# Attention in single hops beside the quantised weight pieces, x and constants issued by SyncE, and another order in the last tile

## The reference, cut to what matters

```python
# layer 0, conditioning: 8 blocks of 32 steps are summed
block_repr = inputs.reshape(B, n_blocks, block_size, H).sum(axis=2)
keys = einsum(block_repr, Wk); keys = keys / rms(keys) * rms_weight
scores = einsum(keys, q); attn = softmax(scores)          # over the blocks
attended = einsum(attn, block_repr)
x0 = layernorm(inputs + attended @ Wo.T) * ln_gamma + ln_beta
# layer 0, feed-forward: activations and weights quantised in blocks of 32
gate, up = q_act(x0) @ q_w(w_gate).T, q_act(x0) @ q_w(w_up).T
x = x + q_act(silu(gate) * up) @ q_w(w_down).T
# layer 1: a GRU over the 256 steps, then a linear layer with a router over 16 experts of rank 16
gi = x_t @ W_ih + b_ih; gh = h @ W_hh + b_hh
r, z = sigmoid(i_r + h_r), sigmoid(i_z + h_z); n = tanh(i_n + r * h_n); h = (1 - z) * n + z * h
out = h @ W.T + bias + sum over the top 2 experts of share * (h @ A.T) @ B.T
x = x + out
```

## Time and profile before

| | us |
|---|---|
| median of 3 runs | 1797.59 |
| lowest, highest | 1797.26, 1799.63 |
| the profiled execution | 1797.46 |
| its span in the trace | 1795.7 |
| busy: PE (matmul) | 1588.7 (88%) |
| busy: DVE | 1448.9 (81%) |
| busy: ACT | 684.1 (38%) |
| busy: POOL | 502.6 (28%) |

### The profile page before, as it was taken

How to read it: one execution, slowest core, us unless ns; L and a number is a source line. 1 busy time by engine, 2 the same in 40 slices (tenths; PEclk the granted TensorE clock), 3 DMA queues, 4 the chain that set the end, 5 groups by cost and what they waited for, 6 DMA issues and landing times.

```text
span 1795.7 us, 76317 instructions
## 1 busy us (share of the span) xinstructions
PE 1588.7 (88%) x32908; PEld 1243.1 (69%) x32908; DVE 1448.9 (81%) x5603; ACT 684.1 (38%) x1736; POOL 502.6 (28%) x572
## 2 busy tenths in 40 slices
PE   5531458999999999999999999999999999999986
PEld 2211126778777777778778777777778777878874
DVE  6968888888888888888888888888888888887654
ACT  2323224444433443444443344443444434443331
POOL 4645323222222222222222222222222222221001
PEclk8755679999999999999999999999999999999996
DMA  8413300000101000001000000000010100000000
GB/s 301 156 66 112 138 18 20 26 33 32 33 32 32 32 32 32 22 19 33 32 32 33 32 33 32 32 28 31 33 33 32 32 32 32 27 27 26 21 15 19
DMA packets 35409, 80.10 MB, mean 45 GB/s; under 512 B 4864, under 2 KB 5248, under 8 KB 34688
## 3 DMA queue, kind: packets, MB, share of 16 engines
q1 hardware_dynamic: 28080, 63.09, 10.3%
q10 hardware_dynamic: 6992, 12.13, 1.9%
HBM read 58.43 MB, written 16.78 MB: 42 GB/s over the span
## 4 chain that ended last, share of the span: by engine, by line
PE 75%; DVE 18%; issue 3%; ACT 2%; POOL 1%; DMA 1%; ACTq 1%; DVEq 0%; SPq 0%; POOLq 0%
PE ps_rn_turn L1274 23%; PE ps_gi L1168 11%; PE ps_z L1274 10%; PE ps_gate_up L1107 6%; PE ps_down L1125 6%; PE ps_base L1177 4%; PE ps_gate_up L1101 4%; PE ps_base L1221 3%; PE ps_route L1177 3%; DVE fe L784 1%; DVE gi L583 1%; DVE gi L585 1%; DVE ps_rn_turn L581 1%; PE ps_rn_turn L1116 1%; DVE ps_gi L566 1%
## 5 line engine op out<-in xcount | busy, mean ns | idle before, releaser
L1274 PE MATMUL ps_rn_turn<-hT,whh 128*128 128x32 f16 x16320 | 449.2, 176 | 37.2 <-DVE hT L722 37.1
L1274 PEld LDWEIGHTS ps_rn_turn<-hT,whh 128*128 128x128 f16 x16320 | 435.2, 96 | 63.8 <-DVE hT L722 56.8
L996 POOL TENSOR_TENSOR qf<-f8c,fe 128x512 bf16<-128x512 bf16 x128 | 135.6, 1059 | 887.2 <-DVE f8c L801 867.3
L1168 PE MATMUL ps_gi<-x1T,wih 128*128 128x128 f16 x4608 | 288.6, 219 | 1.2 <-ACT gi L537 1.2
L1168 PEld LDWEIGHTS ps_gi<-x1T,wih 128*128 128x128 f16 x4608 | 270.2, 98 | 25.6 <-issue 1.7
L546 ACT ACTIVATE r_tanh<-r_pre,scale_half 128x64 f32<-128x64 f32 x256 | 89.0, 348 | 459.2 <-DVE r_pre L742 459.2
L1274 PE MATMUL ps_z<-hT,whh 128*128 128x32 f16 x8160 | 243.2, 176 | 0.0
L1274 PEld LDWEIGHTS ps_z<-hT,whh 128*128 128x128 f16 x8160 | 222.7, 96 | 0.0
L537 ACT ACTIVATE gi<-ps_gi,b_i,scale_x 128x128 f32<-128x128 f32 x384 | 144.4, 456 | 193.2 <-PE ps_gi L1168 193.2
L736 DVE TENSOR_TENSOR r_half<-ps_rn_turn,gi 128x64 f32<-128x64 f32 x256 | 56.5, 221 | 137.9 <-PE ps_rn_turn L1274 137.7
L548 ACT ACTIVATE z_tanh<-z_pre,scale_half 128x64 f32<-128x64 f32 x256 | 89.0, 348 | 159.4 <-DVE z_pre L752 159.4
(11 more groups left out here) (196 smaller groups left out, 2604.5 us busy)
## 6 DMA issues: line engine op xcount, KB each, us to landing
wih<-in_x_steps ACTq DMA_DIRECT2D x32, 256.0 KB, 5.4
xin<-in_x_steps SPq DMA_DIRECT2D x32, 256.0 KB, 3.8
xres<-in_x_steps SPq DMA_DIRECT2D x32, 256.0 KB, 3.2
x_dram<-x SPq DMA_DIRECT2D x32, 256.0 KB, 2.2
x_in<-x_dram SPq DMA_DIRECT2D x32, 256.0 KB, 2.8
out_rows<-y SPq DMA_DIRECT2D x32, 256.0 KB, 2.0
wst<-in_ffn_w SPq DMA_DIRECT2D x12, 512.0 KB, 3.3
sg_gs<-in_ffn_w SPq DMA_DIRECT2D x12, 512.0 KB, 3.8
```

The lines of the kernel that those rows point to most:

```text
L996: g.tensor_tensor(blocked(qf[:, :]), blocked(f8c[:, :]), spread(fe16[:, :]), ALU.mult).then_inc(qf_done, 1)
L1168: last = mm(ps_gi[:, j * P:(j + 1) * P], wih_parts[:, k, at:at + P], x1T[:, x, k, :], start=k + w + x == 0, stop=k == KD - 1 and w == 1)
L1274: last = mm(ps[:, (at + j) * 2 * B:(at + j + 1) * 2 * B], whh[:, k, u, gate * D + j * P:gate * D + (j + 1) * P], hx(t)[:, 2 * k:2 * k + 2, ...
```

## The change

- `over_pieces` has one order for all engines: beside piece p the block sums for p < 8, attention step p-8 for p from 8 to 17 (ten steps), slot (-4, p-18) after that; slots 6 and 7 of c = -4 after the last piece. On ScalarE and SyncE the piece comes first (`piece_first=True`), on the others the work beside it.
- SyncE issues the x tiles (`load_x`), with the same waits on `summed`, and, with piece 4, the constants, `WkT` and `WoT`. ScalarE keeps only the two first constants. The copy to `br` becomes the first attention step of ScalarE.
- Attention has ten steps, one dependent hop in each.
- VectorE's first pass over a piece also waits for its own third pass over the piece before (`w_q`).
- GpSimd's `x_bias` goes from s = 5 to s = 3.
- In the last tile (no R) the base matmuls go from s = 4 and 6 to s = 0 and 3.

```diff
-        def over_pieces(piece, sums, attention, slot, ahead=0):
-            for p in range(SUM_PARTS):
-                sums(p)
-                piece(p // 2, p % 2)
-            for p in range(SUM_PARTS, PIECES // 2):
-                piece(p // 2, p % 2)
-            done = 0
-            for p in range(PIECES // 2, PIECES):
-                upto = min(p - PIECES // 2 + 1 + ahead, 12)
-                for beside in range(done, upto):
-                    if beside < 6:
-                        attention(beside)
-                    else:
-                        slot(-4, beside - 6)
-                    if beside == 11:
-                        slot(-4, 6)
-                        slot(-4, 7)
-                done = upto
-                piece(p // 2, p % 2)
+        def over_pieces(piece, sums, attention, slot, piece_first=False):
+            for p in range(PIECES):
+                if piece_first:
+                    piece(p // 2, p % 2)
+                if p < SUM_PARTS:
+                    sums(p)
+                elif p < SUM_PARTS + ATTENTION:
+                    attention(p - SUM_PARTS)
+                else:
+                    slot(-4, p - SUM_PARTS - ATTENTION)
+                if not piece_first:
+                    piece(p // 2, p % 2)
+            for s in range(PIECES - SUM_PARTS - ATTENTION, STEPS):
+                slot(-4, s)
...
# SyncE
+            def load_x(p):
+                first = (p + 1) * TILES // SUM_PARTS if p else 0
+                for t in range(first, min((p + 2) * TILES // SUM_PARTS, TILES)):
+                    wait(sp, summed, t - XRING + 1)
+                    sp.dma_start(xtile[t % XRING], x_steps[t * P:(t + 1) * P, :]).then_inc(xt_loaded[t % XRING], 16)
+                if p == 4:
...
+                    for dst, src in small:
+                        sp.dma_start(dst, src).then_inc(consts, 16)
+                    sp.dma_start(wk_sb, WkT).then_inc(wkwo_loaded, 16)
+                    sp.dma_start(wo_sb, WoT).then_inc(wkwo_loaded, 16)
-            over_pieces(piece, nothing, nothing, slot)
+            over_pieces(piece, load_x, nothing, slot, piece_first=True)
...
# ScalarE
-            def load_x(p):
...
-                if p == SUM_PARTS - 1:
-                    act.wait_ge(summed, TILES)
-                    nc.scalar.activation(br, ps_down[:, :], ACT.Copy).then_inc(at_act, 1)
             def attention(step):
                 if step == 0:
+                    act.wait_ge(summed, TILES)
+                    nc.scalar.activation(br, ps_down[:, :], ACT.Copy).then_inc(at_act, 1)
+                if step == 1:
                     act.wait_ge(at_pe, 1)
...
-            over_pieces(piece, load_x, attention, slot, ahead=1)
+            over_pieces(piece, nothing, attention, slot, piece_first=True)
...
# VectorE: piece, and the steps of attention (2, 3, 4, 5 become 4, 5, 6, 7)
                 dve.wait_ge(w_abs_ok, count_piece(turn, u, 1))
+                wait(dve, w_q, count_piece(turn, u))
...
# GpSimd (rinv: step 2 becomes 5)
+                if L and s == 3:
+                    pool.wait_ge(x1in_loaded, count(l, 16, 16))
+                    wait(pool, y_ok, count(l, 1))
+                    g.tensor_tensor(x1_bias[:, :], x1_in[:, :], bias_b[:, :], ALU.add).then_inc(x1b_done, 1)
                 if L and s == 5:
...
-                    pool.wait_ge(x1in_loaded, count(l, 16, 16))
-                    wait(pool, y_ok, count(l, 1))
-                    g.tensor_tensor(x1_bias[:, :], x1_in[:, :], bias_b[:, :], ALU.add).then_inc(x1b_done, 1)
...
# TensorE (steps 0, 1, 3, 4, 5 become 1, 2, 5, 6, 7, and the product with WoT step 8)
+            base_parts_at_end = {0: (0,), 3: (1, 2, 3)}
...
                 if L:
-                    for k in base_parts.get(s, ()):
+                    for k in (base_parts if R else base_parts_at_end).get(s, ()):
                         base(l, k)
...
-            over_pieces(piece, block_sums, attention, slot, ahead=1)
+            over_pieces(piece, block_sums, attention, slot)
```

More of the change, by code:

```diff
@@ L50 @@
 SUM_PARTS = 8
+ATTENTION = 10
 PIECE = 1024
@@ L335, in piece @@
                 sp.dma_start(wst[u][:, :], ffn_w[at:at + P, :]).then_inc(w_loaded[u], 16)
+            def load_x(p):
[4 more added lines that the diff above has]
+                if p == 4:
+                    small = [(maskA[:, :], block_mask), (rw_b, rms_w.partition_broadcast(P)),
+                             (q_b, query.partition_broadcast(P)), (iota_b[:, :], iota.partition_broadcast(P)),
+                             (gamma_b[:, :], gamma.partition_broadcast(P)), (beta_b[:, :], beta.partition_broadcast(P)),
+                             (bias_b[:, :], bias.partition_broadcast(P)), (b_i[:, :], b_ih), (b_h[:, :], b_hh),
+                             (rb1_b[:, :], rb1.partition_broadcast(P)),
+                             (rb2_b[:, :], rb2[0:EXPERTS].partition_broadcast(P)),
+                             (gates_b[:, :], gates.partition_broadcast(P)), (rw2_sb[:, :], rw2T)]
+                    assert len(small) == CONSTS
+                    for dst, src in small:
+                        sp.dma_start(dst, src).then_inc(consts, 16)
+                    sp.dma_start(wk_sb, WkT).then_inc(wkwo_loaded, 16)
+                    sp.dma_start(wo_sb, WoT).then_inc(wkwo_loaded, 16)
             def loads(c):
@@ L443, in attention @@
                 if step == 0:
+                    act.wait_ge(summed, TILES)
+                    nc.scalar.activation(br, ps_down[:, :], ACT.Copy).then_inc(at_act, 1)
+                if step == 1:
                     act.wait_ge(at_pe, 1)
                     nc.scalar.activation(brT, ps_route[:, :], ACT.Copy).then_inc(at_act, 1)
[L446 removed]
+                if step == 3:
                     act.wait_ge(at_pe, 2)
                     nc.scalar.activation(keys, ps_base[:, :], ACT.Copy).then_inc(at_act, 1)
[L449 removed]
+                if step == 5:
                     act.wait_ge(at_dve, 8)
                     nc.scalar.activation(row[1], row[0], ACT.Exp).then_inc(at_act, 1)
[L452 removed]
+                if step == 6:
                     act.wait_ge(at_pe, 4)
                     nc.scalar.activation(acol[:, :], ps_base[:, 0:1], ACT.Copy).then_inc(at_act, 1)
[L455 to L460 removed]
+                if step == 7:
+                    act.wait_ge(at_pe, 5)
+                    nc.scalar.activation(attT[:, :], ps_route[:, :], ACT.Copy).then_inc(at_act, 1)
+                if step == 9:
+                    act.wait_ge(at_pe, 6)
+                    nc.scalar.activation(proj[:, :], ps_base[:, :], ACT.Copy).then_inc(at_act, 1)
             def weights(c, s):
@@ L595, in attention @@
                     v.tensor_tensor(b_i[:, 0:2 * KD], b_i[:, 0:2 * KD], b_h[:, 0:2 * KD], ALU.add).then_inc(c_dve, 1)
-                if step == 2:
+                if step == 4:
                     dve.wait_ge(at_act, 3)
@@ L604, in attention @@
                     v.reduce_sum(dot[:, :], kq[:, :], AX_X).then_inc(at_dve, 1)
-                if step == 3:
+                if step == 5:
                     dve.wait_ge(at_pool, 2)
@@ L616, in attention @@
                         .then_inc(at_dve, 1)
-                if step == 4:
+                if step == 6:
                     dve.wait_ge(at_act, 4)
@@ L624, in attention @@
                                     rowr[:, :].unsqueeze(1).broadcast_to([1, BLOCKS, B]), ALU.mult).then_inc(at_dve, 1)
-                if step == 5:
+                if step == 7:
                     dve.wait_ge(at_act, 5)
@@ L957, in attention @@
             def attention(step):
-                if step != 2:
+                if step != 5:
                     return
@@ L1057, in attention @@
             def attention(step):
-                if step == 0:
+                if step == 1:
                     pe.wait_ge(at_act, 1)
@@ L1062, in attention @@
                     last.then_inc(at_pe, 1)
-                if step == 1:
+                if step == 2:
                     pe.wait_ge(wkwo_loaded, 32)
@@ L1081, in attention @@
                     last.then_inc(at_pe, 1)
+                if step == 8:
                     pe.wait_ge(at_act, 6)
```

13 lines of the change are left out of this document (2 added, 11 removed).

## The result

| | before | after |
|---|---|---|
| median of the runs | 1797.59 us (1796.44 to 1799.63, 5 runs) | 1808.24 us (1806.24 to 1811.09, 5 runs) |
| profiled execution, its span | 1797.46, 1795.7 us | 1810.07, 1808.3 us |
| first reduction of `W_hh` | 181.97 us | 196.11 us |
| first state matmul of the loop | 293.56 us | 309.17 us |
| last tile, `ps_route` to `y` | 1778.33 to 1792.47 us | 1793.76 to 1805.08 us |

The ratio is 1.0058, 95% interval [1.0046, 1.007]: slower by 10.65 us between the medians.

The account below looks back on a forecast made before the run. TensorE was taken to bound the loop, VectorE the quantisation stretch before it. Stretch +7.85, end -3.5 and loop +1.0 gave +5.35 on 1797.46: 1802.8 us, range 1793 to 1810.

Parts of the forecast that it names:

- -30.4 us for `w_abs`: Weight quantisation before the loop: VectorE's waits for ScalarE's absolute values go, 7.94 and 22.4 us.
- Start, +1.5: Start: piece 1 loads behind eight x tiles, so the reduction of piece 2 starts at 16.54 instead of 15.02.
- Pieces 3 and 7, 6.8 each: Quantisation: loads of pieces 3 and 7 stand behind SyncE's x-tile waits; VectorE waits 6.8 us for each.
- Piece 5, 21.8: Quantisation: load of piece 5 stands behind x-tile waits and the constants, landing at 61.2; VectorE waits 21.8 us.
- `score`, 1.3: Attention on VectorE: `score` waits 1.3 us for GpSimd's `rinv`, now behind GpSimd's output of piece 12.
- -29.1: Stretch before the loop: 30.4 us of waits for absolute values go, one wait of 1.3 us comes.
- The end, -3.5: Last tile: base matmuls after the logits and a shorter `wxa` let `y` start at 1788.9 instead of 1792.47.
- Drain and loop, +1.0: Full tiles unchanged; in the three tiles before the last, earlier `x_bias` beside the state chain costs 1.0 us net.
- A: Rival: constants are cheap on SyncE, piece 5 lands 8.2 us earlier, total 1794.6 us; chance 0.20.
- B: Rival: SyncE is not late, waits of pieces 3, 5 and 7 come to nothing, total 1767.4 us; chance 0.08.
- C: Rival: `x_bias` holds the state chain in full tiles, 0.6 us in 28 tiles, total 1819.6 us; chance 0.07.
- D: Rival: TensorE's two long attention products stall pieces, up to 5 us each, total up to 1812.8 us; chance 0.07.

Follow-up runs that it names:

- e1: Changed kernel with ScalarE again issuing the x tiles and constants (constants with piece 2), the rest as changed: 1778.52 us, ratio 0.9883.
- e4: Changed kernel with GpSimd's `x_bias` back behind `coeff` in step 5, base matmuls staying as changed: 1809.3 us, ratio 1.0065.
- e5: Changed kernel with the last tile's base matmuls back in their old steps 4 and 6: 1810.08 us, ratio 1.0074.
- e7: Changed kernel with VectorE's `kq` and `score` products written as scalar_tensor_tensor instead of tensor_tensor: 1810.6 us, ratio 1.0061.
- e11: e10 with `kq` reading the key product from PSUM and `score` taking `rinv` as a scalar per partition: 1768.4 us, ratio 0.9834.
- e12: Kernel before with the change's end alone: last tile's base matmuls in steps 0 and 3, `x_bias` in step 3 of every tile: 1795.33 us, ratio 0.9982.
- e10: e8 with `x_bias` back in step 5, in the last tile also behind `wxa`: 1774.38 us, ratio 0.9854.
- e8: e1 with the constants on SyncE, three per place from 1 to 5, `WkT` at place 6, `WoT` at 7: 1773.43 us, ratio 0.9862.
- e2: Changed kernel with SyncE issuing each weight piece two places earlier, ahead of x tiles; constants still one block at place 4: 1784.51 us, ratio 0.9923.
- e3: e2 with the 15 constants and matrices spread, three per place from 1 to 5: 1783.24 us, ratio 0.9919.
- e9: Changed kernel with the constants, `WkT` and `WoT` back on ScalarE at place 2, x tiles staying on SyncE: 1798.95 us, ratio 1.0006.

## Why the prediction was right, and where its terms were off

The sign, the cause and the place were right: slower, because SyncE's waits for x tiles stand in front of weight loads. 1808.24 lies within the range, 5.4 us above the forecast. But the forecast of +5.35 is a small difference of large terms, 36.9 us of late loads against 30.4 of waits won, and the measured difference is twice it. The late loads cost 40.3 us (2.5, 7.43, 22.07 and 8.34). The forecast was 8% short on them; the same too much would have been as likely an error, and would have meant hardly any change. The prediction itself gave slower a chance of 0.55.

- **-30.4 us for `w_abs`.** The waits went to nothing, as said. That it took both parts of the change is shown by e1, where 12.9 us of them are left; with SyncE's part undone the kernel is 20 us faster than before.
- **Start, +1.5.** The reduction of piece 1 waited 3.97 us for its load. In e1 and before the first wait, for `w_abs`, is 1.4, so the start cost about 2.5: the load, issued at 5.22 behind eight x tiles, landed near 12.1 and not at 11.2.
- **Pieces 3 and 7, 6.8 each.** 7.43 and 8.34. Issues at 25.85 and 76.99 against 24.9 and about 75.
- **Piece 5, 21.8.** 22.07. The estimate took the 17.5 us from the first constant's issue to `WoT`'s landing and 1.3 for the piece as one block, 18.8; here it was 63.15 - 45.21 = 17.9.
- **Together** the reduction of piece 9 was to start at 89.4 and did at 92.94: 3.5 us from four terms, each 0.3 to 1.5 us short. In e4, e5 and e7, with the same start, it comes at 92.84, 91.19 and 95.19: late in all four, by 1.8 to 5.8 us, so the terms were short, but their single sizes are good to a microsecond or two only.
- **`score`, 1.3.** 1.26. The chain to `rinv` was right.
- **From piece 9 to `W_hh`.** Here a term was missing. 100.5 us were expected and 103.2 measured: VectorE is held by GpSimd in `kq` and `score`, 1.7 and 1.5 us more than before. The prediction said for -29.1 that the same instructions run on the same engines, and priced only who waits for whom. It had quoted the rule for `wxa` and did not ask it of the attention instructions that the new order sets beside GpSimd's scaling. e11 removes just this.
- **Up to the loop.** 1.5 us between the reduction of `W_hh` and the first state matmul (113.1 against 111.6) were not foreseen. One wait was longer in this execution (2.75 us before):

```profile
238.30 6.73 DVE L646 TENSOR_REDUCE chunk_max<-wih 128x1 f32<-128x1536 f32 x4 [4.53 <-DMA wih<-in_W_ih]
```

  No effect of the change shows in it: in e4, e5 and e7, which have the same code up to there but for `kq` and `score`, it is 2.4 to 2.5 us, and the stretch 111.1, 112.4 and 112.5 us. SyncE's four issues of `W_ih` end 1.1 us later after their first here (10.10 us against 8.99 in those three); why is open.
- **The end, -3.5.** -2.8. `wxa` 0.42 us (0.35 said), the experts' matmuls at a granted clock of 1.00. The missing 0.8 is `x_bias` beside the sum of the logits (0.97 us against 0.18): moving `x_bias` moved the collision. Which instruction it hits there depends on when `x_in` lands; in e12 it was `gap`. e4 shows the trade in the other direction, e10 an end without either.
- **Drain and loop, +1.0.** -0.2, and in e12 nothing either (-0.2). No run shows the 1.0, and with loops that differ by up to 2.4 us between executions none could.
- **The rivals.** A (constants cheap) fell for the changed kernel: piece 5 waited 22.07, not 13.6. e8 shows where it is true. B (SyncE not late) fell by the same rows; e2 shows what it lacked, loads ahead of the waits. C (`x_bias` holds the loop) fell by e12, and the state matmuls of the changed kernel wait 21.3 us between 300 and 1680 us where those before waited 20.8. D (attention stalls pieces by TensorE's products) fell: no wait for `w_abs` is in VectorE's list.

## What to carry to other kernels

Before moving DMA issues to another engine, ask not how long they take but what they wait for and which load stands behind that wait; a load that is needed soon goes ahead of the waiting ones, and large transfers that are needed late are kept out of its way, whoever issues them. When the order of an engine changes, list which of its instructions now run beside GpSimd, and give VectorE's one operand in PSUM or as a scalar per partition. e11 is the kernel to keep: the change's attention order and base matmuls, x tiles on ScalarE, constants spread over SyncE, `x_bias` in step 5 again, in the last tile behind `wxa`, and the two attention products with one tensor operand in SBUF. It takes 1768.4 us, 1.66% under the kernel before.

## What the runs showed of the hardware

- VectorE's instruction with two tensor operands in SBUF, started behind a GpSimd instruction, ends a little after it, and what comes after GpSimd's end grows with its own elements: 0.02 us for 1 element per partition (`score`; `gap` in e12), 0.02 to 0.03 for 8 (`b_i<-b_i,b_h`), 0.04 for 16 (the logits' sum), 0.28 for 256 (`wxa` in e4), 0.54 for 512 (`kq`). That is how it would look if it stood still until GpSimd was done. The cost is what is left of GpSimd's instruction, not a share of its own length: 1.86 us for one element per partition.
- GpSimd's scaling pays too when it starts second: 2.24 us at 119.10, where VectorE's squares, with both operands in SBUF, ran until 119.57, against 1.91 at 129.60.
- A load of 512 KB that is issued right behind some 3 MB of other loads takes over 9 us from issue to landing, at 385 to 406 GB/s, whether the bytes ahead were issued by the same engine (9.1 us, e3) or another (9.3 us, e9).
